# Routing stage and expert stage of a graph-network and mixture-of-experts kernel: input rows added by TensorE in PSUM, routing weights computed later

## The reference, cut to what matters

```python
def reference(x, src, dst, ...):                       # x: 12500 rows of 256 float32, 200000 edges
    edge_index = jnp.stack([src, dst])
    x = x + _L0_gnn_ref(_layernorm(x, axis=-1), edge_index, ...)
    x = x + _L0_ffn_ref(_layernorm(x, axis=-1)[None], ...)[0]
    return x

def _L0_gnn_ref(x, ...):
    out = gcn_conv(x, W1, b1, src, dst, N_NODES)       # messages summed over the edges
    out = jax.nn.relu(batch_norm(out, gamma1, beta1))
    out = gcn_conv(out, W2, b2, src, dst, N_NODES)
    out = batch_norm(out, gamma2, beta2)
    return jax.nn.relu(out + identity)                 # identity: the layer-normed input rows

def _L0_ffn_ref(features, ...):                        # 6 experts, 256 wide, two a row
    rh = jax.nn.relu(features @ router_w1 + router_b1)             # 128 wide
    expert_logits = jax.nn.softmax(rh @ router_w2 + router_b2, axis=-1)
    top_w, top_i = jax.lax.top_k(expert_logits, 2)
    routing_weights = jax.nn.softmax(top_w, axis=-1)
    # per row: the two experts' three layers, weighted by routing_weights and summed
```

## Time and profile before

| | |
|---|---|
| median of three runs | 5498.24 us (5498.19 to 5498.49) |
| profiled execution | 5502.19 us, its span 5500.4 us |
| TensorE busy | 4465.1 us (81%) |
| VectorE busy | 1839.7 us (33%) |
| ScalarE busy | 1203.7 us (22%) |
| GpSimd busy | 3389.7 us (62%) |
| mean granted TensorE clock | 0.726 |
| routing stage | about 4484 to 4760 us of the span |
| counting of tiles, fill rows | about 4760 to 4794 us |
| expert stage | about 4794 us to the end |

### The profile page before, as it was taken

The page is one execution under the profiler, slowest core; times in us unless marked ns, Lnnn a source line. Parts: engine busy times, 40 slices in busy tenths (PEclk is TensorE's granted clock), DMA queues, the critical chain, the costliest instruction groups (busy, mean ns, idle before and its releaser), DMA issues. The chain is left out here.

```text
span 5500.4 us, 79307 instructions
## 1 busy us (share of the span) xinstructions
PE 4465.1 (81%) x15178; PEld 2034.9 (37%) x15179; DVE 1839.7 (33%) x6850; ACT 1203.7 (22%) x2776; POOL 3389.7 (62%) x3633
## 2 busy tenths in 40 slices
PE   5578888888888888777888888878888866499999
PEld 4322222222222222222222222222222234388888
DVE  7422222222222222332222222222222247666665
ACT  6201111111111101230111111111111137455554
POOL 0377777777777777557777777777777734311111
PEclk5677666766777766777666676677666667799999
DMA  4743333333333333353333333333333333411111
GB/s 115 220 134 105 105 105 105 105 105 105 105 105 105 105 105 105 94 148 105 105 105 105 105 105 105 105 105 105 105 105 105 105 85 101 133 50 48 49 49 45
DMA packets 261867, 564.55 MB, mean 103 GB/s; under 512 B 67263, under 2 KB 136225, under 8 KB 261794
## 3 DMA queue, kind: packets, MB, share of 16 engines
q0 software_dynamic: 171264, 466.46, 29.0%
q1 hardware_dynamic: 90530, 97.27, 6.2%
HBM read 503.39 MB, written 60.09 MB: 102 GB/s over the span
## 5 line engine op out<-in xcount | busy, mean ns | idle before, releaser
L638 POOL DMA_INDIRECT ring<-messages,idx_stage x3328 | 3149.5, 946 | 1180.4 <-issue 750.0
L1669 PE MATMUL ps<-ring,onehot_mem 128*64 128x256 f32 x6656 | 2910.0, 545 | 737.1 <-DMA ring<-messages,idx_stage 677.0
L1669 PEld LDWEIGHTS ps<-ring,onehot_mem 128*64 128x64 f32 x6656 | 849.0, 174 | 2437.9 <-DMA ring<-messages,idx_stage 2132.4
L1143 DVE TENSOR_TENSOR acc<-acc,ps 128x128 f32 x832 | 239.8, 288 | 3128.0 <-PE ps L1567 3126.7
L766 ACT ACTIVATE win_rows<-ps 64x256 f32<-64x256 f32 x832 | 313.7, 377 | 1862.8 <-PE ps L1669 1848.2
L1132 DVE TENSOR_SCALAR onehot_mem<-iota_bf,tables 128x64 f32<-128x64 bf16 x3344 | 632.7, 271 | 101.3 <-issue 53.8
L691 POOL DMA_INDIRECT out_dram<-acc x128 | 128.7, 1005 | 597.4 <-DVE acc L1520 416.4
L755 ACT ACTIVATE idx_stage<-tables 128x8 int32 (+1 forms) x420 | 87.4, 209 | 1868.4 <-PE ps L1669 1867.8
L1872 PE MATMUL ps<-acc 128*128 128x256 f32 x2048 | 465.8, 380 | 0.8 <-ACT acc L945 0.8
L1872 PEld LDWEIGHTS ps<-acc 128*128 128x128 f32 x2048 | 384.1, 190 | 53.7 <-issue 1.2
L1567 PEld LDWEIGHTS ps<-ident,win_rows 64*128 64x128 f32 x1664 | 207.9, 175 | 494.6 <-issue 494.6
(11 more groups left out here) (256 smaller groups left out, 2003.6 us busy)
## 6 DMA issues: line engine op xcount, KB each, us to landing
ring<-messages,idx_stage POOLq DMA_INDIRECT x3328, 2.8
rows_mem<-in_x_dram SPq DMA_DIRECT2D x54, 448.0 KB, 4.2
acc<-routed_rows SPq DMA_DIRECT2D x64, 264.0 KB, 3.0
messages<-dinvT SPq DMA_DIRECT2D x23, 448.0 KB, 5.5
dinvT<-in_x_dram SPq DMA_DIRECT2D x22, 448.0 KB, 4.2
messages<-ring SPq DMA_DIRECT2D x19, 448.0 KB, 4.0
dinvT<-dinv_row SPq DMA_DIRECT2D x28, 224.0 KB, 3.4
messages<-rows_mem SPq DMA_DIRECT2D x14, 448.0 KB, 3.8
```

What stands on the lines that cost most here:

```text
L638: pool.indirect_dma_start(out=slots[:, s, :], out_offset=None, in_=t_dram[layer], in_offset=bass.IndirectOffsetOnAxis(ap=idx_stage[:, u, s ...
L1143: dve.tensor_tensor(sums(w, WIN), sums(w, WIN), ps[:, 2 + u, 0:KH * WIN].rearrange("p (k w) -> p k w", k=KH), ALU.add).then_inc(ev_fast, 1)
L1669: pe.matmul(ps[0:WIN, u, 0:D], onehot[:, u, j, 0:WIN], slots[:, s, :], start=j == 0, stop=j == CPG - 1).then_inc(chunks_used, 1)
```

## The change

In the routing stage `turn_z` no longer only transposes `zb`: for each of the four blocks PE first multiplies the identity by the block's `xhat` (256 columns, start of the sum in PSUM), and then multiplies both 128-wide parts of `zb` by the identity as ordinary matmuls that add to it. It now waits for `xhat_done` and for `x1_done` of the chunk two before. `x1_rows` loses its addition and reads the sum from PSUM in its one remaining elementwise instruction. On PE `turn_z(a+2)` stands ahead of `router(a)`. On DVE `places` of a pair moves one step later, between the two `x1_rows` (except in the last three pairs). The two exponentials and the six DVE instructions around them leave the routing stage; the step keeps only the count of ids. The logits (six and the next best) are stored in the routed row in place of the two weights, which makes it 268 values long instead of 264. In the expert stage ACT does `exp_logits` and `exp_gap` and DVE `gap_of` and three instructions more in `keep_ids` for each tile.

```diff
-    ROW = D + 8
+    ROW = D + 4 + NX + 1
+    ROW += ROW % 2
...
             def route(i, q, next1, next2):                       # ACT
...
-                if small:
-                    act.wait_ge(sh_done, i + 1)
-                    hold(act)
-                    act.activation(ex, lg, ACT.Exp).then_inc(ex_done, 1)
                 if next1:
                     norm_x1(i + 1, (q + 1) % XBUFS)
                     keep_xfT(a)
-                if small:
-                    act.wait_ge(gap_done, i + 1)
-                    hold(act)
-                    act.activation(e2, gap, ACT.Exp).then_inc(e2_done, 1)
...
+            def exp_logits(s, u):
+                act.wait_ge(rows_in[u], 16 * (half(s, u) + 1))
+                wait(act, gap_done, s)
+                hold(act)
+                act.activation(ex, tile_rows[u][:, :, X_EXPS], ACT.Exp).then_inc(ex_done, 1)
+
+            def exp_gap(s):
+                act.wait_ge(gap_done, s + 1)
+                wait(act, ids_ready, 2 * s)
+                hold(act)
+                act.activation(e2, gap, ACT.Exp).then_inc(e2_done, 1)
...
             def tile(s, u, next1, next2):                        # ACT
                 hidden(0, s, u, 0)
                 if next1:
                     e0 = expert_of(s + 1, 0)
                     take_hidden(s + 1, 1 - u, 0, e0)
+                    exp_logits(s + 1, 1 - u)
...
                 hidden(1, s, u, 1)
                 if next1:
+                    exp_gap(s + 1)
...
             def x1_rows(t, u, par, p, q):
-                dve.wait_ge(xhat_done, t + 1)
                 dve.wait_ge(z_turned, t + 1)
-                hold(dve)
-                dve.tensor_tensor(xhat[u], rows, xhat[u], ALU.add).then_inc(z_added, 1)
-                dve.wait_ge(z_added, t + 1)
                 wait(dve, routed_out[q], 16 * B2 * (p // XBUFS))
                 hold(dve)
-                dve.scalar_tensor_tensor(out=x1, in0=xhat[u], scalar=0.0, in1=x_in[par][u],
+                dve.scalar_tensor_tensor(out=x1, in0=rows, scalar=0.0, in1=x_in[par][u],
                                          op0=ALU.max, op1=ALU.add).then_inc(x1_done, 1)
...
-            def route2(i):      # three instructions and the wait for ex_done
-            def route3(i, q):   # three instructions and the wait for e2_done; the count of ids stays
...
             def route(i, q, next1, next2):                       # DVE
                 if next1:
                     x1_rows(a, 0, 1 - q % 2, i + 1, (q + 1) % XBUFS)
+                if before:
+                    places(i - 1)
+                if next1:
                     x1_rows(a + 1, 1, 1 - q % 2, i + 1, (q + 1) % XBUFS)
...
                     pair_of(i, q)
-                    route2(i)
-                    route3(i, q)
-                    places(i)
+                    count_ids(q)
                     if not late(i):
+                        places(i)
                         route4(i, q)
...
+            def gap_of(s):      # DVE, expert stage: reduce, reciprocal, one more
             def keep_ids(s, u):
+                dve.wait_ge(e2_done, s + 1)
+                ...             # three instructions: den, first, second
                 dve.wait_ge(expert_a, 2 * s + 1)
                 wait(dve, added[u], 16 * TB * half(s, u))
...
             def turn_z(t, u):
+                pe.wait_ge(xhat_done, t + 1)
                 pe.wait_ge(zb_done, t + 1)
-                wait(pe, z_added, t - 1)
+                wait(pe, x1_done, t - 1)
                 hold(pe)
                 for b in range(BPC):
+                    at = (b % 2) * D
+                    rows = ps[0:RB, 2 * u + b // 2, :]
+                    pe.matmul(rows[:, at:at + D], ident[0:RB, 0:RB], xhat[u][:, b, :], start=True, stop=False)
                     for k in range(KH):
-                        at = (b % 2) * D + k * P
-                        last = turn(ps[0:RB, 2 * u + b // 2, at:at + P], zb[u][:, k, b * RB:(b + 1) * RB])
+                        last = pe.matmul(rows[:, at + k * P:at + (k + 1) * P], zb[u][:, k, b * RB:(b + 1) * RB], ident[:, :],
+                                         start=False, stop=k == KH - 1)
                 last.then_inc(z_turned, 1)
...
             def route(i, q, next1, next2):                       # PE
+                if next2:
+                    turn_z(a + 2, 0)
                 if next1:
                     router(a, 0, (q + 1) % XBUFS)
-                if next2:
-                    turn_z(a + 2, 0)
```

More of the change, by code:

```diff
@@ L138, in gnn_moe @@
         srcT = tables[:, TG * CPG:2 * TG * CPG]
-        ring = sb("ring", [P, max(SLOTS * D, 2 * BPC * (D + 8) + KH * CH)])
+        ring = sb("ring", [P, max(SLOTS * D, 2 * BPC * ROW + KH * CH)])
         onehot_mem = sb("onehot_mem", [P, CPG * GWIN])
@@ L265, in gnn_moe @@
         sum8, dif8, m28, var8 = [old_dinv.take(RB, B2) for _ in range(4)]
-        lg, ex = [old_dinv.take(RB, B2, NX + 1) for _ in range(2)]
         eq, cand, m1st, rest = [old_dinv.take(RB, B2, NX) for _ in range(4)]
         pos, at1 = [old_dinv.take(RB, B2, NDUO) for _ in range(2)]
-        lmax, lsum, lrec, which2, duo, gap, e2, den = [old_dinv.take(RB, B2, 1) for _ in range(8)]
+        lmax, which2, duo = [old_dinv.take(RB, B2, 1) for _ in range(3)]
         node_ids, addr1 = old_dinv.take(RB, B2), old_dinv.take(RB, B2)
@@ L279, in gnn_moe @@
         XBUFS = len(xrow)
-        X_ID, X_FIRST, X_SECOND, X_BEST, X_SHIFT, X_RSTD = [slice(D + n, D + n + 1) for n in range(6)]
+        X_ID, X_BEST, X_SHIFT, X_RSTD = [slice(D + n, D + n + 1) for n in range(4)]
+        X_LOGITS, X_NEXT, X_EXPS = slice(D + 4, D + 4 + NX), slice(D + 4 + NX, D + 5 + NX), slice(D + 4, D + 5 + NX)
         zb = [old_ring.take(P, KH, CH), Region(onehot_mem).take(P, KH, CH)]
@@ L296, in gnn_moe @@
         out_idx = old_acc.take(P, 2, TB).bitcast(I32)
+        ex = old_acc.take(P, TB, NX + 1)
+        lsum, lrec, gap, e2, den = [old_acc.take(P, TB, 1) for _ in range(5)]
+        weights = old_acc.take(P, 2, TB)
         wterm, wsel = old_acc.take(P, 2, 2, TB), old_acc.take(P, 2, 2, TB)
@@ L346, in gnn_moe @@
         sh_done, ex_done, gap_done, e2_done = sem("sh_done"), sem("ex_done"), sem("gap_done"), sem("e2_done")
-        xf_done, z_added = sems("xf_done", 2), sem("z_added")
+        xf_done = sems("xf_done", 2)
         st_done, var_chain, xf_chain, route_chain = sem("st_done"), sem("var_chain"), sem("xf_chain"), sem("route_chain")
+        tile_chain, weights_done = sem("tile_chain"), sem("weights_done")
         pos_done = sem("pos_done")
@@ L885, in route @@
             def route(i, q, next1, next2):
-                a, small = i * 2 + 2, not isinstance(i, int) or i >= 0
+                a = i * 2 + 2
                 if next2:
@@ L976, in _ @@
             take_hidden(0, 0, 1, e1)
+            exp_logits(0, 0)
             keep_xT(0)
+            exp_gap(0)
             take_last(0, 0, 0, e0)
@@ L1374, in route1 @@
                 rstep(dve.scalar_tensor_tensor(out=rest, in0=m1st, scalar=-1e30, in1=lgx, op0=ALU.mult, op1=ALU.add))
-                dve.tensor_reduce(lg[:, :, NX:NX + 1], rest, AX.X, ALU.max).then_inc(sh_done, 1)
+                dve.tensor_reduce(xrow[q][:, :, X_NEXT], rest, AX.X, ALU.max).then_inc(sh_done, 1)
             def pair_of(i, q):
-                first, second = xrow[q][:, :, X_BEST], lg[:, :, NX:NX + 1]
+                first, second = xrow[q][:, :, X_BEST], xrow[q][:, :, X_NEXT]
                 dve.wait_ge(sh_done, i + 1)
@@ L1388, in pair_of, with count_ids @@
                 dve.tensor_tensor(mb_bf, across(duo_mark), duo.to_broadcast([RB, B2, NDUO]), ALU.is_equal).then_inc(mb_ready, 1)
[L1390 to L1405 removed]
+            def count_ids(q):
                 rstep(dve.tensor_scalar(xrow[q][:, :, X_ID], xrow[q][:, :, X_ID], float(XBUFS * 2 * CH), None, ALU.add))
@@ L1501, in norm_rows @@
                 last.then_inc(xh_ready, 1)
-            def keep_ids(s, u):
+            tile_steps = Chain(dve, tile_chain)
+            TILE_STEPS = 4
+            def gap_of(s):
+                tile_steps.begin(s * TILE_STEPS)
+                dve.wait_ge(ex_done, s + 1)
+                hold(dve)
+                tile_steps.step(dve.tensor_reduce(lsum.rearrange("p b o -> p (b o)"), ex[:, :, 0:NX], AX.X, ALU.add))
+                tile_steps.step(dve.reciprocal(lrec, lsum))
+                hold(dve)
+                dve.scalar_tensor_tensor(out=gap, in0=ex[:, :, NX:NX + 1], scalar=-1.0, in1=lrec,
+                                         op0=ALU.add, op1=ALU.mult).then_inc(gap_done, 1)
+            def keep_ids(s, u):
+                dve.wait_ge(e2_done, s + 1)
+                hold(dve)
+                first, second = weights[:, 0, :], weights[:, 1, :]
+                tile_steps.step(dve.tensor_scalar(den, e2, 1.0, None, ALU.add))
+                tile_steps.step(dve.reciprocal(first.unsqueeze(2), den))
+                assert tile_steps.n == TILE_STEPS
```

(7 more changed lines are left out.)

16 lines of the change are left out of this document (3 added, 13 removed).

## The result

The changed kernel takes **5534.16 us** (median of 4 runs, 5530.94 to 5540.27); the kernel before, beside it on the same chip, took 5498.36 (4 runs, 5498.19 to 5503.04). The ratio is 1.0063, with a 95% interval of 1.0051 to 1.0075: 0.6% slower. The profiled execution took 5530.94. The page gives its span and the busy times.

The account below looks back on a forecast made before the run. The routing stage was taken to be bound by VectorE's list, 18.3 us a pair; a TensorE-ScalarE ring of 21.0 replaces it. Eleven distances add 29.7, the start 1.5, in all +31: 5529 us, range 5503 to 5549.

Parts of the forecast that it names:

- The list of VectorE: Routing stage: VectorE's own work per pair, taken as today's longest ring, falls from 18.3 to 12.3 us.
- the ring: Routing stage: longest closed chain of waits; VectorE's 18.3 us a pair gives way to TensorE and ScalarE's 18.96, 21.0 with clock.
- The price of an ordinary product: TensorE's `turn_z`: 0.433 us per 256-column product, 0.22 per 128-column one; the turn 3.49 us at the high clock.
- cheap identity product: Rival, `turn_z`: identity products recorded once, turn 1.75 us, pair 16.5, total 5478 us; chance 0.08.
- dear 128-column product: Rival, `turn_z`: a 128-column product costs as much as a 256-column one, turn 5.2 us, total 5573; chance 0.05.
- The clock: TensorE, routing stage: one fall a step around the first turn, 4.1 us of work at low clock, 2.05 lost.
- stay high (5505): Rival, routing stage: TensorE's clock stays high, the ring is 18.96 us, total 5505 us; chance 0.09.
- low through both turns (5583): Rival, routing stage: clock low through both turns, 26 us a pair, +85, total 5583 us; chance 0.05.
- Pairs: Routing stage: 11 steady distances each grow 21.0 - 18.3 = 2.7 us, 29.7 in all; first and last distances cancel.
- (c), the table loads: ScalarE, routing stage: both exponentials and their table loads go, 13 of 1.283 us before Exp; no saving of its own.
- The expert stage: Added ScalarE and VectorE instructions stay hidden behind TensorE, busy 695 of 705 us; tiles stay 11.0 us apart.
- The cover that was named: Expert stage: VectorE's 1.33 us wait for the previous tile's scatter hides three new instructions; losing it would cost 38 us.

Follow-up runs that it names:

- The fillers: Changed kernel plus five unread 256-column products on TensorE after `router_logits(a + 1)`, run twice: 6388.12 us, ratio 1.0069, and 6287.07 us, ratio 1.0048.
- old_order: Changed kernel with `router(a)` again ahead of `turn_z(a + 2)` on TensorE: 6254.67 us, ratio 0.9997 to the kernel before.
- transposes_2: Changed kernel with the PSUM addition undone (transposes, VectorE's addition), new order and moved exponentials kept, on the usual chip: 5498.78 us, ratio 0.9996.
- exp_only: Kernel before with only the moved exponentials, their six VectorE instructions and late `places`; turn and order as before: 5493.48 us, ratio 0.9986.
- filled_2: Second run of the changed kernel with five unread products on TensorE at the end of each step: 6287.07 us, ratio 1.0048.

## Why the prediction was right

The forecast was +31 us and 5529; measured were +35.8 (medians) and 5534.16, inside the range, and slower as forecast. Point by point:

**Where it would go.** Right. The list of VectorE stopped being the ring, and its gain of 6 us a pair became waits for the turn (93.5 us in the stage). The ring that replaced it is the one derived, link by link. Undoing the turn alone gives all of it back (34.5 us), doing it alone costs more than all of it (+68).

**The price of an ordinary product.** Right. A group of L1804 is two records, one product of 256 columns: it takes 4653.51 - 4653.07 = 0.44. The four records of L1806, two products of 128 columns, take 4653.07 - 4652.63 = 0.44, so 0.22 each. The second turn took 4655.69 - 4652.14 = 3.55 us against 3.49. So a column costs twice what it costs in a transpose (0.22 against 0.11 us for 128 columns), as the prediction took it, and the rivals with the cheap identity product (5478) and the dear 128-column product (5573) fall. The Trainium skill ("Perfetto Trace Analysis", section Transposes) asks that a transpose be done as one. The trace agrees in direction: the turn as ordinary products, together with the products of the identity, cost 34.5 us.

**The ring's links.** Undersized by 0.3 us. Start to start; the third column is the step shown, the last the mean of the 11 steps whose first turns start from 4514.74 to 4727.13:

| link | predicted | step shown | mean of 11 |
|---|---|---|---|
| first turn, with the clock's loss | 3.49 + 2.05 | 5.01 | 5.53 |
| router's transposes to `keep_xfT` | 1.05 | 1.02 | 1.02 |
| `keep_xfT` to `norm_x` | 0.82 | 0.82 | 0.81 |
| `norm_x` to `batch_norm2` | 1.96 | 1.96 | 1.97 |
| `batch_norm2` to second turn | 1.55 | 1.83 | 1.69 |
| second turn | 3.49 | 3.55 | 3.55 |
| logits | 0.72 | 0.71 | 0.72 |
| `router_mm` to `router_hidden` | 1.83 | 1.84 | 1.84 |
| `router_hidden` to `norm_x` | 0.53 | 0.83 | 0.56 |
| `norm_x` to `batch_norm2` | 1.97 | 1.98 | 1.97 |
| `batch_norm2` to first turn | 1.55 | 1.75 | 1.68 |
| sum | 21.01 | 21.30 | 21.32 |

The mis-sized terms are the two hand-overs from ScalarE to TensorE. The prediction took 1.40 + 0.15, the 0.15 from another pair of instructions; they are 1.69 and 1.68 in the mean. The 0.83 of `router_hidden` to `norm_x`, with 0.20 us of pause in it, stands in the step shown alone; nine of the other ten have 0.53.

**The clock.** Right in mechanism and in size, the size in part by luck. The clock falls once a step, just before the first turn (at 4641.09, turn at 4641.50), and of the 13 falls from 4514.79 on it comes back after 3.4 us in 9 and after 6.8 in 4. In the step shown 3.0 us of work ran at the low clock and half of that, 1.5, was lost. Where the low clock lasts 6.8 us nearly the whole turn lies in it. Two lines of PE's timeline show one of these turns, 6.64 us from its start to the router's transposes:

```profile
4576.75 1.16 PE L1804 MATMUL ps<-dinvT,ident 112*112 112x256 f32 x2 [2.60 <-ACT ring L874]
...
4583.39 0.93 PE L1592 MATMUL ps<-ident,rows_mem 112*128 112x112 f32 x8
```

In the mean of the 11 steps the first turn takes 5.53 us, so the loss is 2.04 against the 3.49 of a turn at the high clock, where 2.05 was predicted. The prediction had it as 4.1 us of low clock in every step; it is a mixture of two cases, 1.5 to 1.7 us in eight steps and 2.8 to 3.2 in three. The fillers give the price of the shorter case from the other side, 1.65 us. Both rivals on the clock fall: it doesn't stay high (5505) and isn't low through both turns (5583).

**Pairs.** The 11 steady distances got 21.42 - 18.57 = 2.85 us longer, 31.4 in all (29.7 predicted). Here two errors nearly cancel: the steady distance is 21.4 and not 21.0, and the one before was 18.6; the 18.3 of the prediction is the mean of all 13 between its own marks, whose last one is short. The first got 5.6 shorter and the last 3.7 longer: the prediction let them cancel, and they give -1.9. The start, until the first maximum, got 2.8 longer (+1.5 predicted), and the end of the stage, for which the sum had no term, 2.1. Together 31.4 - 1.9 + 2.8 + 2.1 = 34.4. The range has a loose end: its own bounds were 5514 to 5546, and the last line says 5549 without a term for the 3 us; 5534 lies inside both.

**(c), the table loads.** Right as far as it goes. They have all left the routing stage (13 before Exp and, in the trace of before, 12 before Sqrt, where the prediction had as many), and one of 1.28 us stands before the first tile. These are the timelines of ACT and, last line, PE:

```profile
4822.78 1.28 ACT L959 ACT_TABLE_LOAD   x1 [14.94 <-DMA acc<-routed_rows]
4824.84 0.60 ACT L942 ACTIVATE acc<-ps 128x512 f32<-128x512 f32 x1 [0.55 <-PE ps L1592]
4825.58 7.03 PE L1902 MATMUL ps<-acc 128*128 128x256 f32 x24 [0.84 <-ACT acc L942]
```

It is hidden: what ACT does next is released by PE. That the loads were off the path while they were there is not shown by a run of its own, since the version that moved the exponentials moved both at once.

**The expert stage.** Right: 706.3 to 706.4, with VectorE busy for 488 us of 695 and ScalarE for 391. The cover that was named is still there, as `keep_ids` waits 0.92 us for the scatter (1.33 in the earlier trace rows):

```profile
5139.90 0.61 DVE L1534 SCALAR_TENSOR_TENSOR acc<-acc 128x2 f32<-128x2 f32 x4 [0.92 <-DMA out_dram<-acc]
```

**What the prediction did not see** is how much the parts hang together. It priced the new order only as a part of the new ring. The runs give this ladder of routing stages: before 277.0; PSUM addition alone 345.0; with the exponentials moved 321.5 (old_order, on another chip); with the new order too 311.5. With the long turn the moved exponentials save some 24 us (two chips) and the new order 10 (two chips); with transposes the exponentials save 7.6 (277.0 to 269.4) and the order costs 7.5. The parts can't be priced one at a time and added up.

## What to carry to other kernels

Time saved on one engine counts only up to the next ring: draw the waits as closed rings that pass through several engines, add up each link by link, start to start, and compare the longest before with the longest after. Moving an addition of a few microseconds from VectorE to TensorE isn't free because PSUM adds "for nothing": it turned transposes into ordinary float32 products at twice the time a column and added products of the identity, here 2.6 us a turn where TensorE was already a link. Try a change of several parts in parts; here the one that only moved small work out of the busy stage gained 7 us, and the rest lost 40 (5493.48 to 5533.15).

## What the runs showed of the hardware

- **Less work on TensorE went with a lower clock.** With transposes TensorE's granted clock over the stage was 0.69, with the ordinary products in the same order 0.89. So part of the work taken from TensorE is paid back: the four recorded instructions of `router_mm` take 3.33 us at the low clock (above) and 1.75 at the high one. Products that nobody reads, put into its pause, held the clock high for 37.5 us on end and brought 1.65 us a pair while they did; over the whole stage they gained nothing in any run. The levels are 1.2 and 2.4 GHz. Sums by stretch of `transposes_2`, then of `exp_only`:

```profile
4510.00:4750.00 240.00, 170.16 (x830) 126.72 (x829) 177.84 (x565) 147.34 (x262) 102.17 (x101) 0.69 0.38 114
```
```profile
4510.00:4750.00 240.00, 143.97 (x839) 113.70 (x839) 179.63 (x585) 143.50 (x256) 103.23 (x105) 0.77 0.38 114
```

- With the same work on TensorE, the order alone moved the clock: 0.69 where the turn stands first, 0.77 where it stands behind the router's transposes, and 170 us of busy time instead of 144 for as many instructions. It goes with the 7.5 us that the new order costs with transposes; that the clock is their whole cause isn't shown.
- **Chips differ in how loops run.** On two of the chips used, the kernel before took 750 to 850 us more. Where that time goes is seen in the two versions that were profiled on both kinds of chip. For the transposes' version the routing stage begins 792.5 us later and is 15.5 us longer, 11.6 of them behind the last pair's first maximum; for the addition alone it begins 794 us later and is 2.3 us longer; the expert stage is as long as elsewhere. So nearly all of it lies in the gathering of messages. There several engines stand still together, up to 14 us, and for VectorE's largest wait the profile names no instruction of the core that ended it ("remote"). The waits of `filled_2` and of the kernel before, over the gathering (1000 to 5100 and 1000 to 4400 us), each VectorE's largest:

```profile
DVE acc L1159 <- remote: 1794.1, 265, 13.7
```
```profile
DVE acc L1143 <- PE ps L1567: 2483.1, 652, 6.5
```

What causes these pauses stays open: no run was made for it. Whoever compares versions of a kernel with loops should do so on one chip, and look at the stages before reading a ratio: there the changed kernel in the old order stood at 0.9997, with a routing stage of 321.5 us, and the addition alone at 1.0031 where the usual chip gave 1.0127.
